# A fused two-layer transformer block: the place of the global-key products in the second attention, and the identity products behind them

## The chip, the cores and the metric

The kernel is one program on one core of a Trainium2 chip. The metric is the device time of one execution in microseconds, median of the runs. The engines named below are TensorE (PE, matrix products), VectorE (DVE), ScalarE (ACT), GpSimd (POOL) and SyncE (SP, which issues transfers). Each runs its own list of instructions in order and waits on semaphores that the other engines raise.

## The reference

The input is 16 batches of 256 tokens with 128 features. Four stages follow each other, each with a residual and a layernorm behind it:

```python
x = _layernorm(x + _L0_attn_ref(x, ...))   # 16 heads of 8, rotary, causal
x = _layernorm(x + _L0_ffn_ref(x, ...))    # one of 8 experts (diagonal weights)
x = _layernorm(x + _L1_attn_ref(x, ...))   # the stage that is changed
x = _layernorm(x + _L1_ffn_ref(x, ...))    # two of 8 experts, hidden width 512
```

The second attention has two parts for each of the 16 heads. Each query attends to the keys within 32 positions of it, and, in a softmax of its own, to 25 global keys, whose positions are an input (`global_indices`):

```python
local = softmax(Q Kwindow * scale) Vwindow
Kg, Vg = K[:, global_indices], V[:, global_indices]
glob = softmax(Q Kg * scale) Vg
out = (0.7 * local + 0.3 * glob) @ Wo.T + bo
```

## The kernel before

Both attentions are built by the same functions (`attention_pe`, `attention_act`, `attention_dve`, `attention_pool`, `attention_sp`), with `L.local` true for the second. Its order is written out by hand and unrolled: one iteration i per batch, from -1 to 19, and the iterations overlap. In iteration i the kernel prepares batch i+1 (projection, splitting, stacks of queries and keys), finds the score maxima of batch i (`pass1` on PE, `maxima` on DVE), computes and exponentiates the scores of batches i-1 and i (`pass2` on PE, `exp` on ACT, masks on POOL), multiplies by the values (`pv`), and finishes batch i-2 (`round_ot`, `round_og`, output projection, residual, layernorm). From iteration 4 on, two iterations share the routing of four tiles for the last stage: the even one does the choices on DVE (`chosen`, `both_choices`, L732 to L750), the odd one begins with `round_rp` on PE (L319, L322), which waits for `both_choices`, and with `positions` on DVE, which waits for `round_rp`.

An iteration has four steps j, one for every four heads, and each step has four units u. In unit (j, u) PE does `pass1`(j, u) (two matmuls, L348), then whatever round is due, then `pass2`(j, u), then `pv`(j, u-1). In unit (3, 3) the round is `round_mx(3)` (L172), `pass2` is the scores of the global keys (L372) and `pv` is their product with the values (L404).

The global keys of batch i+1 are picked out of the split keys by `round_kg` (L296): four pairs of matmuls with a selection matrix as the moving operand, 26 columns wide. It needs bank 1 of the two banks that all rounds share, so it waits for the last reader of this bank: ACT's copy of the second key stack, `keep_stack(1, 1)` (L521), which ACT does behind `exp`(3, 2). DVE copies the result to three places (`keep_kg`, L630 twice and L631 once) and raises `kg_kept`. The first `pass1` of the next iteration waits for that.

Behind `round_kg` stands `keep_array_busy` (L331): four fp32 products of the identity with itself, each two passes in the trace, into a bank of scores whose content is no longer needed. They wait for the maxima of unit (3, 2). Their result is read by nobody.

At the start of an iteration ACT copies the output banks (`keep_pv`, L485 and L487), which waits for the last `pv` of the iteration before; PE's `round_ot` (L168) in unit (0, 1) waits for the first of the two copies. ACT's first `exp` of the iteration (L536) comes behind both.

Of the kernel before, what the change touches and what calls it, by code (L numbers as in the profile page):

```python
# [15 lines left out]
P = 128  # L16
# [120 lines left out]
def wait(eng, sem, value):  # L137

    if not isinstance(value, int) or value > 0:
        eng.wait_ge(sem, value)  # L140
# [23 lines left out]
def attention_pe(pe, L, T, W):  # L164


    def turn(out, in_):
        return pe.transpose(out, in_, T.ident[:])  # L168
# [5 lines left out]
    def in_iteration(name, i, p, th):  # L174

        if name in ("og", "vg", "kg", "rt", "rl", "rp") and not L.local:
            return False
        if name in ("rt", "rl", "rp"):
            return th.pair and p == (name == "rp")
        if name in ("ot", "og", "ont", "y"):  # L180
            return th.finish
        if name[:2] == "mx":
            return th.max_step(int(name[2]))
        return th.scores if name == "vg" else th.turn_x if name == "xt" else th.prep
# [28 lines left out]
    def body(i, p, th):  # L213
# [21 lines left out]
        def round_xt(batch, par):  # L235
            if not (isinstance(batch, int) and batch == 0):
                bank_read("xt", i, p, th)
            pe.wait_ge(L.x_in[par], L.x_base + 8 * (batch - par) + 16)
            for tau in range(2):
                m = turn(T.mi[0][:, tau * P:(tau + 1) * P], T.xin[:, par, tau, :])  # L240
            m.then_inc(L.xt_done, 1)
# [8 lines left out]
        def round_pj(tau):  # L250
            bank_read(f"pj{tau}", i, p, th)
            pe.wait_ge(L.xt_kept, i + 2)
            m = pe.matmul(T.mi[tau][:, 0:3 * D], T.xt[:, tau * P:(tau + 1) * P], W.qkv[:], start=True, stop=True)  # L253
            m.then_inc(L.pj_done, 1)

        def round_ont():
            bank_read("ont", i, p, th)
            pe.wait_ge(L.on_done, fin + 1)
            for tau in range(2):
                m = turn(T.mi[0][:, tau * P:(tau + 1) * P], T.on[:, tau, :])  # L260
            m.then_inc(L.ont_done, 1)
# [29 lines left out]
        def round_kg():  # L291
            bank_read("kg", i, p, th)
            pe.wait_ge(L.ts_done, 2 * (i + 1) + 2)
            for t in range(4):
                for kt in range(2):
                    m = pe.matmul(T.mi[1][:, t * 32:t * 32 + NGE], T.tsr[:, kt, (4 + t) * P:(5 + t) * P],  # L296
                                  T.pick[:, kt, :], start=t == 0 and kt == 0, stop=kt == 1, skip_group_check=True)
            m.then_inc(L.kg_done, 1)
# [25 lines left out]
                              start=False, stop=True, skip_group_check=True)  # L324
            m.then_inc(L.rp_done, 2)

        def keep_array_busy():

            wait(pe, L.red_done, L.units * (4 * i + 3) + 3)
            for _ in range(4):  # L330
                pe.matmul(T.s1[0][:, 0:P], T.ident[:], T.ident[:], start=True, stop=True)  # L331

        def pass1(j, u):
            unit = L.units * (4 * i + j) + u
            bank = T.s1[u % L.ring1]
# [95 lines left out]
        for j in range(4):  # L431
            for u in range(L.units):
                if th.scores:
                    pass1(j, u)
                if j == 0 and u == 0 and in_iteration("rp", i, p, th):
                    round_rp()
                if j in (0, 1) and u == 0 and th.prep:
                    round_pj(j)
                if j == 0 and u == 1 and th.finish:
                    round_ot()  # L440
                if j == 0 and u == 2 and th.finish and L.local:
                    round_og()
                if j == 1 and u == (1 if L.local else 0) and th.finish:
                    round_ont()
                if j == 1 and u == 2 and in_iteration("rt", i, p, th):
                    round_rt()
                if j == 2 and u == 1 and L.local and th.scores:
                    round_vg()
                if j == 2 and u == 2 and in_iteration("rl", i, p, th):
                    round_rl()  # L450
                if j == 2 and u == 0 and th.finish:
                    round_y()
                if j == 3 and u in (0, 2) and th.prep:
                    round_stack(1, u // 2)
                if j == 3 and u == 0 and th.turn_x:
                    round_xt(i + 2, p)
                if u == L.units - 1 and th.max_step(j) and not (L.local and j == 0):
                    round_mx(j)
                if th.pass2[j]:
                    pass2(j, u)  # L460
                if th.late and u > 0:
                    pv(j, u - 1)
            if j in (1, 2) and th.prep:
                round_stack(0, j - 1)
            if L.local and j == 0 and th.max_step(j):
                round_mx(j)
        if L.local and th.prep:
            round_kg()
            keep_array_busy()

    iterations(pe, L.local, body)


# [102 lines left out]
def attention_dve(dve, L, T, W, x_all_in=None):  # L576


    def body(i, p, th):
# [44 lines left out]
        def keep_kg():  # L624


            dve.wait_ge(L.kg_done, i + 2)
            kg = T.mi[1][:, 0:4 * 32].rearrange("p (t g) -> p t g", t=4)
            for lo in (0, NGE + S):
                dve.tensor_copy(T.ks[n][:, :, lo:lo + NGE], kg[:, :, 0:NGE])  # L630
            dve.tensor_scalar(T.kg[n][:, :, 0:NG], kg[:, :, 0:NG], T.rows[:, 0:1], None,  # L631
                              ALU.add).then_inc(L.kg_kept, 1)
# [25 lines left out]
        def maxima(j, u):  # L658

            step = 4 * i + j  # L660
            bank = T.s1[u % L.ring1]
            if u == 0:
                wait(dve, L.msp_done, step - 1)
            wait_apart(dve, L.passed, L.p1_done, L.units * step + u + 1)
            nm = T.nm[:, j % 2, 0, :]

            def masked_maximum(item, at, mask):

                return dve.tensor_tensor_reduce(at, at, mask, -1.0, -BIG, ALU.add, ALU.min, nm[:, item:item + 1])  # L669

            if L.local:
                for c in range(2):
                    item = 2 * u + c
                    lo = c * WG + (0 if item // 4 else NGE)
                    masked_maximum(item, bank[:, lo:lo + WIN], T.band[:, item // 4, :])
                lo = 0 if u < 2 else WIN
                m = dve.tensor_reduce(T.nm[:, j % 2, 1, 2 * u:2 * u + 2],  # L677
                                      bank[:, 0:2 * WG].rearrange("p (h k) -> p h k", k=WG)[:, :, lo:lo + NG],
                                      AX.X, ALU.max, negate=True)
            elif u == 0:  # L680
                for t in range(4):
                    m = masked_maximum(t, bank[:, t * P:(t + 1) * P], T.causal[:, P:S])
            else:
                for c in range(2):
                    m = masked_maximum(2 + 2 * u + c, bank[:, c * S:(c + 1) * S], T.causal[:, :])
            m.then_inc(L.red_done, 1)
# [96 lines left out]
        for j in range(4):  # L783
            for u in range(L.units):
                if th.scores:
                    maxima(j, u)
                if second_half and j == 0:
                    if u == 0:
                        positions()
                    if u == 1:  # L790
                        places()
                    if u == 3:
                        weights_of_choices()
                if first_half:
                    if (j, u) == (2, 3):
                        logits()
                        best_of(T.best[:, :], 1)
                    if (j, u) == (3, 0):
                        chosen(0, 4)
                        without_first()  # L800
                    if (j, u) == (3, 1):
                        best_of(T.best2[:, :], 7)
                    if (j, u) == (3, 3):
                        chosen(1, 10)
                        both_choices()
                if j in (0, 1) and u == 0 and th.prep:
                    keep_pj(j)
                if j == 0 and u == L.units - 2 and th.finish:
                    normalise()
                if j == 2 and u == (2 if L.local else 0) and th.finish:  # L810
                    residual()
                if j == 2 and u == 1 and L.local and th.scores:
                    keep_vg()
                if j == 3 and u == 2 and th.finish:
                    layernorm()
        if L.local and th.prep:
            keep_kg()

    iterations(dve, L.local, body)

# [1231 lines left out]
```

## Time and profile before

| what | value |
|---|---|
| median of 3 runs | 1143.39 us (1137.0, 1143.39, 1153.99) |
| the profiled execution's own time | 1135.99 us |
| its span, first to last instruction | 1134.2 us |
| PE busy in the span | 960.8 us (85%) |
| DVE, POOL, ACT busy | 770.9, 666.2, 579.3 us |
| second attention | from about 450 to about 905 us of the span |

The times in the rows below are microseconds from the start of the span, durations microseconds (ns only where marked). A timeline row gives the start, the length, the engine, the line, the operation and how many instructions were merged; in brackets the idle time before it and what ended it. Lengths of matmuls overlap, because they are pipelined: the cost of a group is the distance from its start to the start of the next group.

### The profile page before, as it was taken

To read this page: it belongs to the slowest core of one execution; us is meant where nothing else is said; L and a number is where in the kernel's file an instruction comes from. 1 tells how busy PE (TensorE), PEld (TensorE's weight loads), DVE (VectorE), ACT (ScalarE), POOL (GpSimd) and SP (SyncE) were. 2 spreads that over 40 slices of the span, in tenths; PEclk is the share of its full clock that TensorE was granted. 3 is DMA by queue.
4 is the path that set the end of the run, shared out by engine and by line. 5 is a ranking of instruction groups with operands and counts; after the bars stand their busy time and mean duration, and the time that the engine had idled before them with its cause. 6 is when DMAs were issued, how large, how long until landed. Compare 5 with 4: busy or idle time off the path is not lost.

```text
span 1134.2 us, 27975 instructions
## 1 busy us (share of the span) xinstructions
PE 960.8 (85%) x7664; PEld 711.1 (63%) x7664; DVE 770.9 (68%) x3598; ACT 579.3 (51%) x1250; POOL 666.2 (59%) x1493
## 2 busy tenths in 40 slices
PE   3899999999959995899999999999999419999930
PEld 2667777777735552777777777777776318888720
DVE  3877778788826785567677767677775327777736
ACT  2566666666622332355555455554545107777724
POOL 3566666566632222267668787787778522565556
PEclk8999999999978998599999999999999559999965
DMA  6111111211032432111112121211211157777636
GB/s 179 37 40 44 29 44 29 48 25 44 22 132 95 179 125 84 44 32 28 47 30 57 37 55 45 63 42 55 58 33 35 45 166 230 238 256 249 207 96 163
DMA packets 71377, 98.36 MB, mean 87 GB/s; under 512 B 13689, under 2 KB 43257, under 8 KB 71105
## 3 DMA queue, kind: packets, MB, share of 16 engines
q1 hardware_dynamic: 61040, 83.31, 25.0%
q0 software_dynamic: 4992, 10.30, 2.6%
q10 hardware_dynamic: 5232, 3.42, 1.2%
q8 instruction: 50, 0.82, 0.3%
q14 instruction: 63, 0.51, 0.1%
HBM read 49.48 MB, written 24.77 MB: 65 GB/s over the span
## 4 chain that ended last, share of the span: by engine, by line
PE 71%; DVE 11%; issue 5%; DMA 4%; POOL 3%; ACT 3%; SPq 2%; ACTq 0%; DVEq 0%; POOLq 0%
PE bank L348 6%; PE bank L172 5%; PE bank L253 4%; PE bank L357 4%; PE bank L378 4%; PE bank L1262 4%; PE bank L412 3%; PE bank L168 3%; PE bank L419 3%; PE bank L1496 3%; PE bank L1497 3%; PE bank L1498 3%; PE bank L352 3%; PE bank L387 3%; PE bank L404 3%
## 5 line engine op out<-in xcount | busy, mean ns | idle before, releaser
L536 ACT ACTIVATE p<-bank 128x480 f32<-128x480 f32 (+1 forms) x448 | 239.8, 539 | 271.8 <-PE bank L378 108.4
L669 DVE CUSTOM_DVE_ANT_0 bank<-bank,band 128x160 f32<-128x160 f32 x512 | 156.8, 347 | 91.8 <-PE bank L348 90.2
L669 DVE CUSTOM_DVE_ANT_0 bank<-bank,causal 128x128 f32<-128x128 f32 (+1 forms) x512 | 169.4, 386 | 65.3 <-PE bank L352 51.8
L898 POOL TENSOR_SCALAR_AFFINE_SELECT p<-p 128x380 f32<-128x380 f32 (+1 forms) x256 | 146.3, 601 | 75.7 <-ACT p L536 74.9
L669 DVE DVE_READ_ACCUMULATOR2_ANT nm<- 128x1 f32 x1024 | 143.9, 141 | 0.1
L1675 POOL DMA_INDIRECT y_rows<-p,rows x92 | 90.1, 979 | 83.6 <-DVE p L1622 61.9
L879 POOL TENSOR_SCALAR_AFFINE_SELECT p<-p 128x256 f32<-128x256 f32 (+1 forms) x192 | 90.7, 484 | 64.2 <-ACT p L536 60.9
L348 PE MATMUL bank<-ks,qs 128*128 128x186 f32 x512 | 117.2, 313 | 1.3 <-DVE nm L677 1.1
L348 PEld LDWEIGHTS bank<-ks,qs 128*128 128x128 f32 x512 | 80.4, 198 | 34.0 <-issue 19.3
L378 PE MATMUL bank<-qs,ks 128*128 128x160 f32 x512 | 101.0, 300 | 0.0
L1617 DVE TENSOR_TENSOR ks<-p,ts 128x512 fp32r<-128x512 f32 x92 | 63.9, 694 | 28.4 <-ACT ts L1570 26.7
L1567 ACT ACTIVATE p<-bank,wb 128x512 f32<-128x512 f32 x92 | 63.6, 691 | 37.9 <-PE bank L1498 35.6
L928 POOL DMA_INDIRECT xr<-xs,placei x64 | 65.0, 1016 | 27.1 <-DVE xs L779 15.2
L378 PEld LDWEIGHTS bank<-qs,ks 128*128 128x128 f32 x512 | 75.2, 193 | 7.5
L172 PE MATMUL bank<-identr,ts 128*128 128x128 f32 x512 | 71.0, 265 | 8.0 <-POOL ts L869 6.5
L172 PEld LDWEIGHTS bank<-identr,ts 128*128 128x128 f32 x512 | 55.2, 146 | 20.8 <-issue 12.4
L1262 PE MATMUL bank<-p,expert 128*128 128x512 f32 x128 | 67.0, 607 | 0.7 <-DVE p L1321 0.7
L412 PE MATMUL bank<-p,vb 128*32 128x160 f32 x1024 | 61.3, 311 | 1.1 <-POOL vb L835 0.6
L357 PE MATMUL bank<-ks,qs 128*128 128x256 f32 x256 | 61.9, 325 | 0.3 <-DVE nm L669 0.3
L253 PE MATMUL bank<-w_qkv,xt 128*128 128x384 f32 x128 | 59.6, 553 | 1.0 <-ACT xt L492 1.0
L352 PE MATMUL bank<-ks,qs 128*128 128x128 f32 x256 | 42.0, 288 | 19.3 <-ACT ks L521 14.7
L357 PEld LDWEIGHTS bank<-ks,qs 128*128 128x128 f32 x256 | 39.1, 193 | 26.2 <-issue 24.5
(209 smaller groups left out, 2370.0 us busy)
## 6 DMA issues: line engine op xcount, KB each, us to landing
qs<-parts SPq DMA_DIRECT2D x46, 512.0 KB, 5.2
qs<-qf SPq DMA_DIRECT2D x128, 128.0 KB, 2.4
rows<-xr SPq DMA_DIRECT2D x23, 260.0 KB, 3.2
parts<-ks SPq DMA_DIRECT2D x8, 512.0 KB, 2.7
xs<-x_b SPq DMA_DIRECT2D x16, 256.0 KB, 2.9
p<-in_w SPq DMA_DIRECT2D x12, 256.0 KB, 3.2
xin<-in_x SPq DMA_DIRECT2D x16, 128.0 KB, 2.2
parts<-qf SPq DMA_DIRECT2D x4, 512.0 KB, 2.7
```

The source lines that it names most:

```text
L172: return pe.transpose(out.bitcast(F32R), in_, T.identr[:])
L253: m = pe.matmul(T.mi[tau][:, 0:3 * D], T.xt[:, tau * P:(tau + 1) * P], W.qkv[:], start=True, stop=True)
L348: m = pe.matmul(bank[:, c * WG:(c + 1) * WG], q[:, t, tau * P:(tau + 1) * P], k[:, t, lo:lo + WG], start=c == 0, stop=True, skip_group_che ...
L357: m = pe.matmul(bank[:, c * S:(c + 1) * S], q[:, t, P:S], k[:, t, NGE:NGE + S], start=c == 0, stop=True, skip_group_check=True)
L378: m = pe.matmul(bank[:, c * WIN:(c + 1) * WIN], k[:, t, NGE + kt * P:NGE + (kt + 1) * P], q[:, t, lo:lo + WIN], start=c == 0, stop=True, s ...
L412: m = pe.matmul(T.ov[32 * t:32 * t + 32, lo:lo + WIN], T.vb[n][:, part, j, t, :], flat[:, item * WIN:(item + 1) * WIN], start=j == 0 and p ...
L536: act.activation(pb[:, :, :].rearrange("p u c -> p (u c)")[:, lo:lo + cols], bank[:, 0:cols], ACT.Exp, scale=SCALE).then_inc(L.exp_done, 1)
L669: return dve.tensor_tensor_reduce(at, at, mask, -1.0, -BIG, ALU.add, ALU.min, nm[:, item:item + 1])
L879: pool.affine_select(out=at, in_=at, compare_op=ALU.is_ge, fill=0.0, base=0, pattern=[[0, heads], [1, P]], channel_multiplier=-1).then_inc ...
L898: pool.affine_select(out=at, in_=at, compare_op=ALU.is_ge, fill=0.0, base=base, pattern=[[0, 4], [sign, hi - lo]], channel_multiplier=-sig ...
L1262: pe.matmul(T.yb[p][:, :], W.expert[:, e * D:(e + 1) * D], T.xm[e % 4], start=e == 0, stop=e == E - 1).then_inc(M.y_done, 1)
L1675: pool.indirect_dma_start(Z.y_dram[:, :], bass.IndirectOffsetOnAxis(ap=rows[:, a, C_GOAL:C_GOAL + 1].bitcast(I32), axis=0), Z.ys[r][:, a * ...
```

## The change

Three things change, all in the second attention. PE's `round_kg` moves from the end of the iteration into unit (3, 3), behind `pass1`(3, 3) and ahead of `round_mx(3)`, `pass2`(3, 3) and `pv`(3, 2). DVE's `keep_kg` moves from the end of the iteration to the place right behind `maxima(3, 3)`; in the even iterations from 4 on this is ahead of `chosen` and `both_choices`, in all others nothing stood between. `keep_array_busy` is removed. No transfer is added, removed or moved, and the lists of ACT, POOL and SP stay as they are.

```diff
-        def keep_array_busy():
-
-            wait(pe, L.red_done, L.units * (4 * i + 3) + 3)
-            for _ in range(4):
-                pe.matmul(T.s1[0][:, 0:P], T.ident[:], T.ident[:], start=True, stop=True)
 ...
                 if j == 3 and u == 0 and th.turn_x:
                     round_xt(i + 2, p)
+                if L.local and (j, u) == (3, 3) and th.prep:
+                    round_kg()
                 if u == L.units - 1 and th.max_step(j) and not (L.local and j == 0):
                     round_mx(j)
                 if th.pass2[j]:
 ...
-        if L.local and th.prep:
-            round_kg()
-            keep_array_busy()
 ...
                 if th.scores:
                     maxima(j, u)
+                if L.local and (j, u) == (3, 3) and th.prep:
+                    keep_kg()
 ...
-        if L.local and th.prep:
-            keep_kg()
```

## Rows read from the trace of the kernel before

**Rows 1.** Page: granted TensorE clock in 40 slices, tenths of full speed.
```profile
PEclk8999999999978998599999999999999559999965
```

**Rows 2.** Windows: busy time per engine (instructions), granted clock, DMA share, GB/s.
```profile
640.00:740.00 100.00, 96.51 (x918) 72.12 (x919) 73.22 (x434) 53.84 (x128) 80.69 (x200) 0.98 0.18 50
```

**Rows 3.** Waits of PE from 480 to 880: total us, times, longest.
```profile
PE bank L172 <- DVE logits L719: 7.1, 6, 1.2
PE bank L172 <- DVE on L610: 3.0, 15, 0.3
```

**Rows 4.** Timeline of PE, end of iteration 5 and start of 6.
```profile
603.02 0.47 PE L348 MATMUL bank<-ks,qs 128*128 128x186 f32 x2
603.32 0.28 PE L172 MATMUL bank<-identr,msp 128*16 128x128 f32 x2
...
604.45 1.15 PE L296 MATMUL bank<-pick,ts 128*128 128x26 f32 x8
605.45 1.14 PE L331 MATMUL bank<-ident 128*128 128x128 f32 x8
606.40 0.44 PE L348 MATMUL bank<-ks,qs 128*128 128x186 f32 x2
...
607.88 0.49 PE L168 MATMUL bank<-ident,ovs 128*128 128x128 f32 x3
```

**Rows 5.** Timeline of ACT, the same stretch.
```profile
603.05 0.59 ACT L521 CAST ks<-bank 128x512 fp32r<-128x512 f32 x1
...
604.84 0.58 ACT L485 COPY ovs<-bank 128x512 f32<-128x512 f32 x1
605.32 0.59 ACT L487 COPY ogs<-bank 128x512 f32<-128x512 f32 x1
607.85 0.57 ACT L536 ACTIVATE p<-bank 128x480 f32<-128x480 f32 x1 [1.94 <-PE bank L378]
```

**Rows 6.** Timeline of DVE, the same stretch.
```profile
604.75 0.20 DVE L677 TENSOR_REDUCE nm<-bank 128x2 f32<-128x50 f32 x1
605.63 0.44 DVE L630 CAST ks<-bank 128x104 fp32r<-128x104 f32 x2 [0.69 <-PE bank L296]
605.99 0.31 DVE L631 TENSOR_SCALAR kg<-bank,rows 128x100 f32<-128x100 f32 x1
```

**Rows 7.** Timelines of DVE and PE, end of iteration 4 (even).
```profile
579.08 0.20 DVE L677 TENSOR_REDUCE nm<-bank 128x2 f32<-128x50 f32 x1
...
579.79 0.24 DVE L749 TENSOR_TENSOR both<-picks 128x32 f32<-128x32 f32 x1
577.62 0.47 PE L348 MATMUL bank<-ks,qs 128*128 128x186 f32 x2
...
581.28 0.33 PE L319 MATMUL bank<-both,tri 128*128 128x32 f32 x2
```

**Rows 8.** Timeline, end of iteration -1 (the array at half clock).
```profile
462.04 0.31 DVE L631 TENSOR_SCALAR kg<-bank,rows 128x100 f32<-128x100 f32 x1
...
463.20 0.71 PE L348 MATMUL bank<-ks,qs 128*128 128x186 f32 x2
```

**Rows 9.** Timeline, end of iteration 0.
```profile
480.39 0.58 ACT L521 CAST ks<-bank 128x512 fp32r<-128x512 f32 x1
...
481.02 1.06 PE L296 MATMUL bank<-pick,ts 128*128 128x26 f32 x8
```

**Rows 10.** Windows, columns as in rows 2: two stretches with waits.
```profile
624.00:628.00 4.00, 3.48 (x20) 2.23 (x21) 1.04 (x8) 1.09 (x3) 3.64 (x11) 0.58 0.01 5
868.00:872.00 4.00, 3.38 (x39) 2.32 (x39) 1.68 (x5) 2.12 (x5) 3.71 (x13) 1.00 0.47 135
```

**Rows 11.** Timeline of PE: identity products ending iterations 6, 7 and 8.
```profile
633.63 1.14 PE L331 MATMUL bank<-ident 128*128 128x128 f32 x8
658.99 1.14 PE L331 MATMUL bank<-ident 128*128 128x128 f32 x8
685.97 1.14 PE L331 MATMUL bank<-ident 128*128 128x128 f32 x8
```

## The prediction

> **What bounds the kernel now.** I read the page's slices first: between the second expert stage and the last one the granted clock stands at 9 tenths or more for some ten slices, and drops to 5 at either end [rows 1]. That plateau is the second attention. The windows over it show why: in 100 us PE is busy for 96.51, POOL for 80.69, DVE for 73.22, ACT for 53.84 [rows 2]. So in this stage PE's own list of instructions is the bound, and a product that is taken off the list is worth its full distance to the next one, unless PE then has to stand still for another engine. The waits of PE confirm it: from 480 to 880 there are two kinds that repeat, 7.1 us in 6 waits and 3.0 us in 15 [rows 3], some 10 us in 400. Both are answered by DVE chains that start from PE's own `pass1`, so they move along with PE and neither swallow nor return a gain.
>
> **The identity products.** In steady state they start at 605.45 and the next `pass1` at 606.40 [rows 4]: 0.95 us for the group, 16 groups in the trace (iterations -1 to 14). DVE copies the keys during them: it ends at 605.99 + 0.31 = 606.30 [rows 6], 0.10 us before the `pass1`. So the identity products cover the copy, and taking them out alone would win about 0.1 us a batch. The gain hangs on the other half of the change.
>
> **The moved products, on PE.** I count from s, the start of `pass1`(3, 3), here 603.02. In the old order `round_mx(3)` starts at s+0.30, the key products at s+1.43, the identity products at s+2.43, the next `pass1` at s+3.38 [rows 4]. In the new order the key products want to start at s+0.30. They need the copy of the second key stack, which ACT runs from 603.05 for 0.59 us [rows 5], until s+0.62. PE follows about 0.05 us behind such an end: at iteration 0 the copy ends at 480.39 + 0.58 = 480.97 and the key products start at 481.02 [rows 9]. So they start at s+0.67, and PE stands for up to 0.37 us that it did not stand before. Queued behind this wait are `round_mx(3)`, `pass2`(3, 3) and `pv`(3, 2). The key products take 1.00 us (604.45 to 605.45), the three behind them 1.13 us (603.32 to 604.45) [rows 4]. The next `pass1` could be at s+0.67+1.00+1.13 = s+2.80. That is 0.58 us earlier than now. The bounds of this term: if ACT's copy came first there would be no wait and the gain would be 0.95; if the copy is as late as in iteration 0, nothing is left.
>
> **The keys' copy, on DVE.** The first copy starts 605.63 - 604.45 = 1.18 us behind the start of the key products and the last one ends 0.67 us later [rows 4, 6], so in the new order at s+0.67+1.18+0.67 = s+2.52. The maxima of unit (3, 3) end at 604.95, s+1.93 [rows 6], and the copies behind them at s+2.60 at the latest. Both are ahead of s+2.80, so `pass1` does not wait for `kg_kept`. The margin is 0.2 to 0.3 us. It is the new cover: the maxima row, `pass2` and `pv` in place of the identities.
>
> **Even iterations from 4 on.** Here `chosen` and `both_choices` stand behind the copies. Now they run from the end of the maxima, 579.28, to 580.03: 0.75 us. In the new order they run from s+2.52 (maxima end at s+1.66) to about s+3.3, with wake-ups s+3.4. `round_rp` started at s+3.66 (581.28 less 577.62) [rows 7] and would be ready at s+3.08. It stands for about 0.3 us, and of the 0.58 some 0.25 is left. There are six of these (4, 6, ..., 14). What is behind `round_rp` on PE, the projection and `pass2`(0, 0), moves with it.
>
> **The ends.** At iteration -1 the key products are in the same place and only the identities go. DVE ends at 462.35 and `pass1` starts at 463.20 [rows 8]; it can start near 462.40: 0.8 us, at half clock. At iteration 0 the key products already start at the end of ACT's copy [rows 9]; the copies on DVE then end 1.85 us later at 482.87, about where `pass1` starts now. I count 0.05.
>
> **What loses slack and costs nothing.** `pv`(3, 2) is the last product of the iteration, and ACT's copies of the output banks wait for it. In the old order it ended a little before 604.84, the first copy ran then for 0.58, and `round_ot` came at 607.88 [rows 4, 5]: 2.5 us to spare. In the new order `pv` ends 1.37 us later and `round_ot` comes 0.58 us earlier, which leaves about 0.5. Likewise ACT is free for `exp`(0, 0) at 605.91 now and waits 1.94 us for it [rows 5]; 1.94 - 1.37 - 0.58 is zero. Both covers still hold, by little. If they went, the cost would be tenths of a microsecond in eight batches. No transfer is moved; the row of maxima that SyncE sends for `round_mx(3)` leaves 1.3 us later and is needed only in step 1 of the next iteration. The wait of the identity products for the maxima of (3, 2) goes too, but the next `pass1` has the same wait.
>
> **The sum.** 8 x 0.58 = 4.6 (iterations 1, 2, 3, 5, 7, 9, 11, 13), 6 x 0.25 = 1.5, 0.8 and 0.05: 7.0 us. The profiled execution took 1135.99; by the sum it would take 1129. The median of the runs is 7.4 us above it, and the four times shown (with the profiled one) have their middle at 1140.2. I take that middle: 1140.2 - 7.0 = 1133.
>
> **Clock: rule against row.** In the trace the array falls to its lower level (1.2 of 2.4 GHz) at times behind DVE's long wait: the window at 624 has a granted clock of 0.58 [rows 10], and the iteration with it takes 28.18 us from identity to identity (605.45 to 633.63), where the same kind without a fall takes 26.98 (658.99 to 685.97) [rows 4, 11]. A fall costs 1.2 us. The stretch at 868, where PE is idle for 0.6 of 4 us in pieces, keeps a clock of 1.00 [rows 10], and so do the fifteen short waits of 0.2 to 0.3 us [rows 3]. The new waits (0.37 and 0.3) are of this size, so I count no new falls. The Trainium skill, TensorE: Matmul & The Clock Gate, section "A second HAM failure mode: psum-queue depth-cycling", speaks against the change: it says that a PE which idles for moments between groups of matmuls, often enough, has its clock swing between the two levels and pays for each swing. By that rule the second rival below would be the likely one. The trace, with its fifteen short waits and no fall at them, does not agree with it at this size of wait.
>
> **Rivals.** (1) The forecast above, 1133: chance 0.57. (2) Slower: the clock falls at the batch boundary. The wait of 0.37 us and 1.0 us of products only 26 columns wide follow each other, and no identities of 128 columns come behind. Price 1.2 us a fall. It decides from six falls on, which eat the 7.0; at all 15 boundaries with scores it is +18 - 7 = +11, so 1151. For it: the old order never has a wait right before the narrow products. Against it: the rows just told. Chance 0.17. (3) A wait takes the gain: ACT's copy comes later (as in iteration 0), or `pass1` waits for `kg_kept` as DVE is late behind a layernorm. Then the 0.58 shrinks to 0.1 or 0.2 and the sum is about 3 us or less: 1137 to 1140. For it: margins of 0.2 us. Against: the rows of one boundary recur nearly to the hundredth. This is also the case in which the change does not do what it says. Chance 0.17. (4) More: PE waits for nothing new, 15 x 0.95 + 0.8 = 15 us, or some of the old falls vanish too (1.2 each): 1125 to 1130. Chance 0.09.
>
> **Numbers.** The range has to take in the executions' own spread, 1136 to 1154 before the change, as well as the cases: from 1125 (case 4) to 1151 (case 2). A difference of 2% is 23 us, about what a measurement of this kernel can tell from no change. No case reaches it: faster would take the whole of case 4 and a lucky median, 0.04; slower would take some 25 falls, 0.04; within 2%: 0.92.
>
> **What would show it.** Right: the interval from `pass1`(3, 3) to the next `pass1` is 2.8 us in place of 3.38; L296 follows L348 after about 0.67 us with an idle time ended by ACT's L521; L319 shows a wait of some 0.3 us for L749 in six iterations; PE's busy time is some 16 us lower, and the span only some 7. Wrong: `pass1` waits for L631, the granted clock falls between iterations, or `round_ot` waits for L485. The forecast is wrong as a whole if the stage's time between two boundaries does not fall by 0.2 to 0.6 us in iterations without a clock fall.

## The result: 1.9% slower, and the profile after

| | before | after |
|---|---|---|
| median of 6 runs | 1143.46 us | 1163.45 us |
| lowest, highest | 1136.31, 1153.99 | 1160.04, 1198.72 |
| ratio after to before | | 1.0194, 95% interval 1.0138 to 1.025 |
| profiled execution, span | 1134.2 us | 1158.7 us |
| mean granted clock over the span | 0.920 | 0.903 |

Ratios leave disturbed executions out, medians here and below hold all of them, so the two can give different distances (in e10 below 16 and 25 us). The forecast was 1133 with a range up to 1151: the time went the other way and lies outside the range. In the changed kernel the line numbers are lower: `pass1` L342, `pass2` of the global keys L366, `pv` L398 and L406, ACT's key copy L513, `both_choices` L741; `round_kg` is still L296.

The page's clock row, beside that of before [rows 1]:

```profile
PEclk9999999999979996699888799888999659999975
```

The plateau of the second attention now has sixes, sevens and eights in it. A stretch in which the granted clock is at its lower level, 1.2 of 2.4 GHz, is called a fall; the batch boundary is the stretch from `pass1`(3, 3) to the first `pass1` of the next iteration. Two windows give it as one number: first the second attention of the kernel before, from its first to its last `pass1`, then that of the changed kernel (columns as in rows 2).

```profile
463.20:865.60 402.40, 389.73 (x3643) 293.99 (x3643) 291.48 (x1746) 208.16 (x493) 294.06 (x766) 0.97 0.16 43
```
```profile
462.41:886.20 423.79, 407.77 (x3522) 301.74 (x3522) 291.75 (x1748) 208.53 (x493) 295.50 (x766) 0.89 0.15 41
```

The stage is 21.4 us longer (423.8 less 402.4) with 121 matmuls fewer in the records; PE's busy time rose by 18 us, DVE, ACT and POOL do what they did. The granted clock went from 0.97 to 0.89. Summed over windows of 2 us, the full-speed time lost to the clock (length times one less the clock, "clock loss" from here on) is 12.4 us before and 45.0 after. The span grew by 24.5; the other 3 us lie outside the stage, where the loop of the last stage alone took 5 us longer (144.9 against 140.0 us). That is not the change's: e10, the changed kernel again, has 139.1.

The batch boundary itself went as the diff says. Timeline of PE in the changed kernel, end of iteration 9 (columns as in rows 4):

```profile
722.99 0.47 PE L342 MATMUL bank<-ks,qs 128*128 128x186 f32 x2
723.65 1.06 PE L296 MATMUL bank<-pick,ts 128*128 128x26 f32 x8 [0.20 <-issue]
724.57 0.28 PE L172 MATMUL bank<-identr,msp 128*16 128x128 f32 x2
...
725.70 0.55 PE L342 MATMUL bank<-ks,qs 128*128 128x186 f32 x2
726.17 0.91 PE L253 MATMUL bank<-w_qkv,xt 128*128 128x384 f32 x2
```

From `pass1`(3, 3) to the next `pass1` it is 2.71 us; it was 3.38 [rows 4]. The iteration's length at full clock, from 700.69 to 725.70, is 25.01 us; the odd iterations of before take 25.37. So each boundary is shorter, and the stage is longer. Windows of the changed kernel around the end of iteration 6 show where it goes:

```profile
628.00:632.00 4.00, 2.75 (x32) 2.04 (x24) 3.35 (x22) 0.81 (x2) 3.56 (x6) 0.87 0.05 17
632.00:636.00 4.00, 4.00 (x25) 2.83 (x24) 0.86 (x5) 1.21 (x3) 3.11 (x10) 0.50 0.04 10
636.00:640.00 4.00, 4.00 (x25) 3.26 (x24) 2.56 (x19) 1.80 (x4) 0.54 (x1) 0.50 0.63 148
640.00:644.00 4.00, 4.00 (x29) 2.68 (x28) 2.23 (x14) 0.92 (x2) 3.14 (x12) 0.50 0.00 0
644.00:648.00 4.00, 4.00 (x19) 3.61 (x16) 1.24 (x9) 1.70 (x4) 1.17 (x2) 0.50 0.16 54
648.00:652.00 4.00, 4.00 (x23) 3.04 (x22) 2.15 (x13) 0.88 (x2) 0.00 (x0) 0.57 0.03 6
```

PE stands for 1.25 us in the first window: the old wait for DVE's choices. In the unit ahead of it stand the router's products, 8 columns wide, so that narrow products and a wait come close together here as at the new boundary (timeline of PE in the changed kernel):

```profile
628.41 1.02 PE L311 MATMUL bank<-router,xrt 128*128 128x8 f32 x8
...
630.06 0.46 PE L342 MATMUL bank<-ks,qs 128*128 128x186 f32 x2
631.77 0.38 PE L172 MATMUL bank<-identr,msp 128*16 128x128 f32 x2 [1.25 <-DVE logits L711]
```

Then the clock falls to its lower level and stays there for 20 us although PE shows 4.00 busy of 4.00. In the kernel before such a fall was over after some 3.5 us [rows 10]. The changed kernel has eight falls between 480 and 884: two of 20 us, one of 10, two of 7, three of 3.5. Five of them start in unit (2, 3), at or just behind the old wait for the choices, and three at the boundary, behind the moved key products. The kernel before had three of 3.5, all of which start in unit (2, 3).

The waits of PE from 480 to 900 in the changed kernel (columns as in rows 3):

```profile
PE bank L172 <- DVE logits L711: 7.3, 6, 1.2
PE bank L172 <- DVE on L602: 2.9, 14, 0.3
PE bank L296 <- ACT ks L513: 2.2, 8, 0.8
PE bank L296 <- issue: 1.0, 5, 0.2
...
PE bank L319 <- DVE both L741: 0.2, 1, 0.2
```

New are the waits ahead of the key products, 3.2 us in 13. As idle time they cannot carry 21 us. The wait for `both_choices`, forecast for six iterations, occurs once.

### The profile page after: what moved, and what is told of

It reads as the page before. It is cut to its first block, busy times and chain, and to the rows that moved or that the text cites. A ratio compares the mean times of both kernels' runs of the same rounds, so it can differ in the third digit from the quotient of the medians.

```text
span 1158.7 us, 27719 instructions
## 1 busy us (share of the span) xinstructions
PE 978.0 (84%) x7536; PEld 715.8 (62%) x7536; DVE 769.9 (66%) x3598; ACT 578.3 (50%) x1250; POOL 670.6 (58%) x1493
## 3 DMA queue, kind: packets, MB, share of 16 engines
q1 hardware_dynamic: 61040, 83.31, 24.5%
## 4 chain that ended last, share of the span: by engine, by line
PE 69%; DVE 11%; issue 7%; ACT 4%; POOL 3%; SPq 3%; DMA 2%; another core or an unknown queue 1%; ACTq 0%; DVEq 0%; POOLq 0%
PE bank L342 6%; PE bank L172 5%; PE bank L253 4%; PE bank L372 4%; PE bank L351 4%; PE bank L1254 3%; PE bank L168 3%; PE bank L413 3%; PE bank L1488 3%; PE bank L1490 3%; PE bank L406 3%; PE bank L1489 3%; PE bank L346 3%; PE bank L381 3%; PE bank L398 3%
## 5 line engine op out<-in xcount | busy, mean ns | idle before, releaser
L1667 POOL DMA_INDIRECT y_rows<-p,rows x92 | 92.5, 1005 | 87.2 <-DVE p L1614 60.7
L342 PE MATMUL bank<-ks,qs 128*128 128x186 f32 x512 | 124.2, 328 | 2.3 <-DVE nm L669 1.4
L342 PEld LDWEIGHTS bank<-ks,qs 128*128 128x128 f32 x512 | 86.1, 208 | 38.6 <-issue 22.7
L372 PE MATMUL bank<-qs,ks 128*128 128x160 f32 x512 | 107.9, 316 | 0.0
L372 PEld LDWEIGHTS bank<-qs,ks 128*128 128x128 f32 x512 | 81.0, 206 | 9.2 <-issue 3.0
L253 PE MATMUL bank<-w_qkv,xt 128*128 128x384 f32 x128 | 63.4, 585 | 1.1 <-ACT xt L484 1.0
L406 PE MATMUL bank<-p,vb 128*32 128x160 f32 x1024 | 63.2, 320 | 0.9 <-POOL vb L827 0.5
L381 PE MATMUL bank<-qs,ks 128*128 128x256 f32 x256 | 55.8, 299 | 0.0
```

What stands on the lines that cost most here:

```text
L342: m = pe.matmul(bank[:, c * WG:(c + 1) * WG], q[:, t, tau * P:(tau + 1) * P], k[:, t, lo:lo + WG], start=c == 0, stop=True, skip_group_che ...
L372: m = pe.matmul(bank[:, c * WIN:(c + 1) * WIN], k[:, t, NGE + kt * P:NGE + (kt + 1) * P], q[:, t, lo:lo + WIN], start=c == 0, stop=True, s ...
L406: m = pe.matmul(T.ov[32 * t:32 * t + 32, lo:lo + WIN], T.vb[n][:, part, j, t, :], flat[:, item * WIN:(item + 1) * WIN], start=j == 0 and p ...
L1667: pool.indirect_dma_start(Z.y_dram[:, :], bass.IndirectOffsetOnAxis(ap=rows[:, a, C_GOAL:C_GOAL + 1].bitcast(I32), axis=0), Z.ys[r][:, a * ...
```

## The experiments

Two theories. **C**, clock: the identity products kept the array active; without them the clock falls more often and stays down longer. **S**, schedule: the new order puts work behind waits on PE and DVE, and that costs the time. All runs are in groups on one chip with the kernel before beside them. The expectations give absolute times, those of e1, e2, e3 and e6 for a kernel before of some 1143 us, the others for some 1135; where the kernel before of the group took another time, they are read as distances from it.

| run | median us | before, median | ratio (95% interval) | clock loss, stage us (one profile) | median clock of the runs |
|---|---|---|---|---|---|
| e10, changed kernel again | 1159.71 | 1134.98 | 1.0144 (1.0106 to 1.0182) | 52.1, 429.9 | 0.896 |
| e1, before without products | 1149.15 | 1136.49 | 1.0113 (1.0079 to 1.0148) | 50.2, 433.4 | 0.909 |
| e2, moved, products at the end | 1151.71 | 1136.49 | 1.0140 (1.0103 to 1.0176) | 22.9, 417.5 | 0.915 |
| e3, moved, products ahead of the keys | 1137.12 | 1136.49 | 1.0015 (0.9989 to 1.0042) | 25.1, 413.5 | 0.922 |
| e6, before, products 8 columns wide | 1143.67 | 1136.49 | 1.0072 (1.0046 to 1.0099) | 29.1, 417.4 | 0.914 |
| e4, before, choice waits filled | 1130.70 | 1134.98 | 0.9958 (0.9941 to 0.9976) | 5.0, 397.8 | 0.932 |
| e5, changed, choice waits filled | 1134.38 | 1134.98 | 0.9977 (0.9951 to 1.0003) | 13.4, 398.8 | 0.922 |
| e9, changed, two ahead, filled | 1127.52 | 1134.98 | 0.9936 (0.9913 to 0.9959) | 7.6, 394.5 | 0.927 |
| e12, changed, filled 8 columns wide | 1161.95 | 1143.47 | 1.0101 (1.0029 to 1.0173) | 44.8, 423.6 | 0.895 |
| e8, before without products, filled | 1147.26 | 1143.47 | 1.0045 (1.0008 to 1.0082) | 20.5, 410.6 | 0.919 |
| e11, changed, four ahead, filled | 1142.96 | 1143.47 | 0.9958 (0.9915 to 1.0001) | 9.6, 402.1 | 0.931 |

The median clock of the kernel before in the three groups was 0.926 (e1, e2, e3, e6), 0.925 (e10, e4, e5, e9) and 0.923 (e12, e8, e11). The profiles of e1, e3, e6, e8 and e10 fell on executions of 1169.3, 1149.6, 1150.1, 1153.8 and 1165.0 us, which lie 20, 12, 6, 7 and 5 us above their medians. Above all in e1 and e3 the clock of the profile (0.891 and 0.911) is lower than in a usual execution of the kernel, so the last column is the one to compare.

**e1: take the products out, move nothing.**

```diff
             round_kg()
-            keep_array_busy()
```

> The kernel before with the identity products left out and nothing moved. Theory C (clock): without them TensorE's clock falls at batch boundaries and stays down longer; the clock time lost in the second attention rises from 5 us at full speed (three falls of 3.4 us) to 20 to 40, and the time is 10 to 22 us above the kernel before (1153 to 1165). Theory S (schedule: the new waits at the moved key products and on VectorE cost the time): nothing is moved here, so the time is that of the kernel before less about 1 us (1142), since VectorE's copy covers all but 0.1 us of the products.

Measured: 1.0113. This is 13 us above before, as C has it (10 to 22), and S is excluded as the whole cause, as no instruction is moved. The full-clock iterations show that the products cost nothing where they stood. In the timeline of PE in e1 at the end of iteration 5 the distance from `pass1` to `pass1` is 3.38 as before; the time of the products has become waiting. The second fence, of the waits of PE from 480 to 895, shows this at all 15 boundaries:

```profile
607.38 0.46 PE L348 MATMUL bank<-ks,qs 128*128 128x186 f32 x2
...
608.81 1.15 PE L296 MATMUL bank<-pick,ts 128*128 128x26 f32 x8
610.76 0.43 PE L348 MATMUL bank<-ks,qs 128*128 128x186 f32 x2 [0.81 <-issue]
```
```profile
PE bank L348 <- issue: 13.0, 15, 1.2
```

And a window of the same execution (at 1169.3 us the second slowest of e1), in which the clock is down nearly throughout with PE busy for 22.05 of 24 us:

```profile
796.00:820.00 24.00, 22.05 (x119) 16.84 (x118) 10.71 (x66) 6.86 (x16) 10.08 (x27) 0.51 0.14 36
```

**e2: keep the moves, products at the end of the iteration.**

```diff
             if L.local and j == 0 and th.max_step(j):
                 round_mx(j)
+        if L.local and th.prep:
+            keep_array_busy()
```

> The changed kernel with the four identity products put back at the end of the iteration (the moves stay). Theory C: the falls go back to about three, the boundary from pass1(3,3) to the next pass1 is 2.71 + 0.95 = 3.66 us against 3.38 before, so the time is 2 to 5 us above the kernel before (1145 to 1149). Theory S: the moves are what costs, so it stays at 1160 or above.

Measured: 1.0140, 15 us, against 2 to 5 expected by C. The time met neither theory: it is 10 us above C's, and S wanted 1160 or above. The boundary is 3.71 us (3.66 expected); that is about 5 us of work over 15 boundaries. The rest goes with the clock: 0.915 against 0.926, and the profile has falls that touch the boundaries of iterations 0, 4 and 12. The longest, 17 us, starts at the wait for the choices of iteration 12. So products in the old place do not make up for the moved keys. That it is their distance from the narrow key products and from the wait ahead of them is argued and not shown.

**e3: keep the moves, products ahead of the keys.**

```diff
                 if L.local and (j, u) == (3, 3) and th.prep:
+                    keep_array_busy()
                     round_kg()
```

> The changed kernel with the four identity products put ahead of the moved key products in unit (3, 3), where 0.37 us of them fill the wait for ScalarE's copy. Theory C: few falls, boundary 0.30 + 0.95 + 1.00 + 1.13 = 3.38 us as before, time within 4 us of the kernel before (1140 to 1147). Theory S: as the changed kernel, 1160 or above. If falls come back although the products are there, their place right behind the narrow products is what counts.

Measured: 1.0015, no difference from before. With the products in the wait, the moved keys, the new order on DVE and the later copies on ACT are all still there, and the 20 us are gone. S falls with this run. The boundary is 3.16 us (3.38 expected), and the odd iterations take 25.41 (before 25.37). The profile, of an execution 12 us above the median, still has a fall of 20 us. It starts at the wait for the choices of iteration 14 and runs through the boundary, wide products and all:

```profile
844.00:848.00 4.00, 3.33 (x23) 2.53 (x23) 1.33 (x10) 1.21 (x3) 3.64 (x11) 0.69 0.01 4
848.00:852.00 4.00, 4.00 (x25) 3.31 (x24) 2.87 (x21) 1.62 (x3) 0.94 (x2) 0.50 0.64 148
...
860.00:864.00 4.00, 4.00 (x20) 3.96 (x19) 1.88 (x15) 0.88 (x2) 0.00 (x0) 0.50 0.01 4
864.00:868.00 4.00, 4.00 (x36) 2.56 (x36) 2.55 (x13) 1.23 (x4) 1.46 (x3) 0.75 0.03 6
```

**e6: the old kernel, products 8 columns wide.**

```diff
-                pe.matmul(T.s1[0][:, 0:P], T.ident[:], T.ident[:], start=True, stop=True)
+                pe.matmul(T.s1[0][:, 0:8], T.ident[:], T.ident[:, 0:8], start=True, stop=True)
```

> The kernel before with the identity products cut from 128 to 8 moving columns (8 of the identity's columns, same number of instructions, same place). If what keeps the clock is that the array works on many columns (theory C in its strict form), the falls come as in the changed kernel: 1153 to 1165. If it is enough that TensorE executes something, or if the schedule is the cause (S), it stays at 1140 to 1145, like the kernel before.

Measured: 1.0072, between the two cases. The iterations at full clock are as before (26.98, 25.37 us), so the 7 us are clock. It leaves open whether narrow products at the boundary help by half or not at all: its interval overlaps that of e1. e12 asks the same in the other place.

**e10: the changed kernel again.** No edit.

> The changed kernel once more, on the chip of this group, for its clock and span run by run. Theory C (clock): about 20 to 27 us above the kernel before, and over the runs of both kernels the time goes up by 0.7 us for each microsecond of full-speed clock time lost; at equal loss the changed kernel is 4 to 7 us faster. Theory S (schedule): at equal loss it is still 10 us or more slower.

Measured: 1159.71 against 1134.98, 25 us in the medians and 16 by the ratio (C expected 20 to 27). That the changed kernel is slower holds on another chip. The clock loss over the whole span has a median of 120.4 us against 85.0 for before, 35.4 more. Over the six runs of this kernel the time goes up by 0.89 us per microsecond of clock loss (0.71 over the first six), and over the 24 of before by 0.52, over the 17 of the other group by 0.71. In the stage alone, e10 and e5 (below) differ in little but the clock, as e5's added products stand in waits: (429.9 - 398.8) / (52.1 - 13.4) = 0.80. With 0.8, a clock loss of 35.4 us costs 28, and the measured 24.7 would leave a gain of 3 to 4 us at equal clock, where C expected 4 to 7. This estimate hangs on the slope: with 0.52 it is a loss of 6 us, with 0.89 a gain of 7. e5 against e4, below, measures the gain without it.

**e4 and e5: fill the waits for the choices**, in before and in the changed kernel.

```diff
+        def fill_choice_wait(n):
+            wait(pe, L.red_done, L.units * (4 * i + 2) + 3)
+            for _ in range(n):
+                pe.matmul(T.s1[0][:, 0:P], T.ident[:], T.ident[:], start=True, stop=True)
 ...
+                if (j, u) == (2, 3) and th.scores and in_iteration("rl", i, p, th):
+                    fill_choice_wait(4)
                 if u == L.units - 1 and th.max_step(j) and not (L.local and j == 0):
                     round_mx(j)
```

> The kernel before, with four more identity products (0.95 us) in the six waits of 1.1 to 1.2 us in unit (2, 3) of the even iterations, where TensorE stands for VectorE's choices. They write a score bank whose maxima are done. Theory C: the falls that begin at these waits go away (three in the trace of before, 1.2 us each): 1 to 6 us faster than the kernel before (1131 to 1135). Theory S: idle time of TensorE does not matter, no change.

> The changed kernel with the same four products in the same six waits; the batch boundary stays without products. Theory C: the falls that begin at the waits, and run on through the boundary for up to 20 us, go away; those that begin at the boundary itself (three in the trace) stay: 8 to 18 us faster than the changed kernel, still 3 to 15 us above the kernel before. Theory S: as the changed kernel.

Measured: e4 0.9958, 4.3 us faster than before, and its profile has no fall between 480 and 880 (one of 7 us from 472). e5 0.9977: 25 us faster than the changed kernel in the medians, 19 by the ratios, where C expected 8 to 18, by products in six waits that lie elsewhere. Timeline of PE in e5, unit (2, 3) of iteration 6; the wait for L719 shrinks from 1.2 to 0.32 us:

```profile
629.99 0.47 PE L348 MATMUL bank<-ks,qs 128*128 128x186 f32 x2
630.29 1.08 PE L331 MATMUL bank<-ident 128*128 128x128 f32 x8
631.69 0.28 PE L172 MATMUL bank<-identr,msp 128*16 128x128 f32 x2 [0.32 <-DVE logits L719]
631.91 0.64 PE L372 MATMUL bank<-qs,kg 128*32 128x256 f32 x8
```

e4 and e5 have all iterations from 2 to 14 at full clock, so they give the schedule's gain cleanly: 23.86 against 24.25 us in iteration 3, 25.01 against 25.37 in the odd and 26.61 against 26.98 in the even ones, 0.37 a batch. Still the medians order them the other way (1134.4, 1130.7): e5's clock is 0.922 against 0.932, and its profile has a fall of 10 us that starts at the boundary of iteration 0. At the other 14 boundaries with scores none starts.

**e12: the same fill, 8 columns wide.**

```diff
-                pe.matmul(T.s1[0][:, 0:P], T.ident[:], T.ident[:], start=True, stop=True)
+                pe.matmul(T.s1[0][:, 0:8], T.ident[:], T.ident[:, 0:8], start=True, stop=True)
```

> The changed kernel with four products in the waits for the choices, as in the run before, but 8 moving columns wide in place of 128. If the array's activity (columns) is what holds the clock, the falls at these waits stay and the time is 10 to 25 us above the kernel before (1145 to 1160). If any executed matmul holds it, the time is that of the changed kernel with wide products in the waits, within 2 us of the kernel before (1133 to 1137).

Measured: 1161.95, 18 us above before in the medians and 12 by the ratio (interval 3 to 20), as the activity case has it (10 to 25). The median clock, 0.895, is that of the changed kernel without any fill (0.896); with the wide fill it was 0.922. Timeline of PE in e12, the same unit:

```profile
636.24 0.47 PE L348 MATMUL bank<-ks,qs 128*128 128x186 f32 x2
636.54 1.13 PE L331 MATMUL bank<-ident 128*128 128x8 f32 x8
637.91 0.38 PE L172 MATMUL bank<-identr,msp 128*16 128x128 f32 x2 [0.24 <-DVE logits L719]
638.23 1.08 PE L372 MATMUL bank<-qs,kg 128*32 128x256 f32 x8
```

and its windows over the same stretch:

```profile
636.00:640.00 4.00, 3.76 (x31) 2.34 (x23) 2.39 (x14) 1.00 (x3) 3.38 (x10) 0.65 0.01 2
640.00:644.00 4.00, 4.00 (x26) 3.66 (x28) 1.69 (x11) 1.66 (x4) 1.45 (x3) 0.50 0.33 78
...
652.00:656.00 4.00, 4.00 (x16) 3.39 (x16) 1.63 (x9) 0.69 (x2) 0.00 (x0) 0.50 0.19 60
656.00:660.00 4.00, 4.00 (x35) 3.18 (x34) 2.58 (x18) 1.67 (x4) 0.63 (x2) 0.79 0.00 0
```

The narrow products occupy PE as long as the wide ones (1.13 and 1.08 us in the profile) and leave as short a wait (0.24 and 0.32), and the clock falls all the same and stays down for 20 us. So in these waits busy time in the profile does not hold the clock, and the width of the products does.

**e8: before without the boundary products, waits filled.** The edits of e1 and e4 together.

> The kernel before without the identity products at the batch boundary, with four wide products in the waits for the choices. Theory C with a start and a continuation (falls start at the waits for the choices, and the products at the boundary end them early): filling the waits leaves few starts, so the missing boundary products cost little: 1130 to 1136, against 1149 without the fill. If falls start at the boundary as often: 1140 to 1150.

Measured: 1.0045, 1147.26, 3.8 us above before in its group, which itself was 7 to 8.5 us slower than the other two groups. As a distance from before it lies between the two cases. Its profile has the second one's falls: one of 10 us and five of 3.5, all starting within 2.6 us behind the first `pass1` after a boundary, where e4, with the products, has none. Filling the waits removes the long falls of e1 but not the starts at the boundary, where e8 has key products of 26 columns and a wait of 0.81 us behind them. One of the six, at the end of iteration 6, in a timeline of PE and a window:

```profile
641.38 1.15 PE L296 MATMUL bank<-pick,ts 128*128 128x26 f32 x8
643.33 0.43 PE L354 MATMUL bank<-ks,qs 128*128 128x186 f32 x2 [0.81 <-issue]
```
```profile
644.00:648.00 4.00, 4.00 (x21) 3.40 (x20) 2.36 (x15) 0.57 (x1) 0.79 (x1) 0.60 0.11 33
```

**e9 and e11: the better version.** Changed kernel, fill of e5, and two or four wide products ahead of the key products.

```diff
                 if L.local and (j, u) == (3, 3) and th.prep:
+                    keep_array_busy(2)   # e11: 4
                     round_kg()
```

> The changed kernel with two identity products (0.48 us) ahead of the moved key products, where 0.37 us is a wait, and the four in the waits for the choices. Theory C: boundary about 2.9 us (before 3.38), few falls: 2 to 8 us faster than the kernel before, if two products are enough to hold the clock; between the two kernels if not. Theory S: 1160 or above.

> As the best version so far (moved key products, products ahead of them, waits for the choices filled), with four products ahead in place of two. Boundary 3.16 us in place of 2.72, so 15 x 0.44 = 6.6 us more work if the two already hold the clock: 1133 to 1135. If the two leave falls that four would prevent: 1128 or below.

Measured: e9 0.9936, 7.5 us faster than before, and 32 us (by the ratios 24) faster than the changed kernel in its group: it beats both. About 6 of the 7.5 us are what the moved keys save at full clock (below), so this is mostly the schedule's gain, with the clock held. Against e5, which lacks only the two products, it is 7 us faster. Timeline of PE in e9 (here `pass1` is L354), end of iteration 7:

```profile
653.26 0.47 PE L354 MATMUL bank<-ks,qs 128*128 128x186 f32 x2
653.56 0.63 PE L331 MATMUL bank<-ident 128*128 128x128 f32 x4
653.95 1.04 PE L296 MATMUL bank<-pick,ts 128*128 128x26 f32 x8
...
655.98 0.55 PE L354 MATMUL bank<-ks,qs 128*128 128x186 f32 x2
```

The boundary is 2.72 us, that of the changed kernel (2.71): the two products stand wholly in the wait for ACT's copy. e11's boundary is 3.16. Its median clock is 0.931 against 0.923 for before in its group (e9 0.927 against 0.925), its stage takes 402.1 us against 394.5, and its ratio 0.9958 (0.9915 to 1.0001) lies 0.2% above e9's, 2.5 us where 6.6 were expected; the intervals overlap, so the order of the two is not settled.

## Why the prediction was wrong

**What bounds the kernel: right.** PE's list is the bound, and its time per product is the time. That is also why the clock weighs so much: 0.8 us of stage time for each microsecond of clock loss.

**The schedule steps: right in kind, 0.4 instead of 0.58 and 0.25.** The key products start at s+0.66 (s+0.67 forecast), the next `pass1` at s+2.71 (s+2.80). Behind it stands 0.2 us that I had not: L253 follows 0.47 us behind `pass1` and not 0.28. In the even iterations the wait for `both_choices` (0.3) does not appear, since DVE's copies start 0.1 us earlier than taken and the routing steps behind them take 0.74 us. What remains is 0.37 us a batch in all kinds (e5 against e4), about 5.3 us over iterations 1 to 14, and the 0.8 at iteration -1, where `pass1` now starts 0.09 us behind the copy [rows 8]. The sum was 7.0; by these it is about 6. The covers that were to hold by little held: `round_ot` waits for no copy in these iterations.

**The step that failed: "I count no new falls".** The forecast put this term at nothing; the stage's clock loss went from 12.4 to 45.0 us, in eight falls for three. I asked only whether the new waits would start one, and priced a fall at 1.2 us from a kernel in which falls were short. First, falls do start at the changed boundary: three of the eight. The fifteen short waits without a fall [rows 3] stood ahead of products of 128 columns, not ahead of 26-column ones. Second, the old waits for the choices start falls anyway, three of six before and five of six after, and a fall from there has no fixed length. In the changed kernel two of the five run 20 us, through the next boundary, and one of 7 us is followed by one of 10 over the boundary; the other two last 3.5. Together the falls cost some 26 us (0.8 times 32.6), less a gain of about 5, which is the 21.4 by which the stage grew. e1 shows that missing products alone cost clock and time, e3 that the moves with products ahead of them do not, and e5 that without the starting waits nearly all of the loss is gone.

**What ends a fall is not shown.** In the kernel before, the three falls were over some 5 us ahead of the boundary's products: the first ends at 628.0, the products start at 633.63 [rows 11]. So these products did not end them. Over the profiles of all runs, 31 falls start in unit (2, 3). The 14 that start within 1.5 us behind its `pass1`, before the wait there ends, last 7 to 27 us; of the 17 that start later, 16 last 3.5 us and one, in e3, 20. The one profile of the kernel before has only late ones. How much of the lengthening is owed to the missing products, and how much to the place in the wait at which a fall happened to begin, these traces do not separate. That the products hold the clock rests on the clock over all runs (0.926 to 0.909 in e1) and on the starts at the boundary (six in e8, none in e4 from 480 to 880).

**The rivals.** Rival 2 named the clock and its reason, the missing wide products behind a wait and narrow products, with 0.17. It had the place by less than half, as five of the eight falls start at the old waits, and its size (+11) was too small, as the price of 1.2 us a fall was. The Trainium skill's rule in TensorE: Matmul & The Clock Gate, section "A second HAM failure mode: psum-queue depth-cycling", that small idle times between groups of matmuls make the clock swing, was weighed and set aside. By that rule, the trace of the changed kernel agrees, with eight falls for three. The rule speaks of idle time only; in e12 the narrow products left the clock where the bare waits had left it (0.895 and 0.896).

**What stays open.** Whether a given wait starts a fall varies between executions and batches (three of six waits before), and no run shows what decides it. Why the products protect the boundary ahead of the keys (e3) and hardly at the end of the iteration (e2) is argued from their distance to the narrow products and not shown. The gain of the moved keys at equal clock is read from one profile each of e4 and e5. The last stage's loop takes 138.4 to 140.0 us in some profiles and 143.2 to 145.5 in others (changed kernel, e12, e8, e11) with the same code, so the first comparison's 5 us there are not the change's.

## What to carry to other kernels

Before products without a reader are deleted, ask what the clock does without them; test the deletion alone, and read the granted clock per window, not PE's busy time. If a kernel is bound by TensorE, put wide idle products into waits that exist anyway, ahead of narrow products: there they cost nothing (2.72 against 2.71 us at the boundary). Here they bring 0.4% to the kernel before (e4), and to the changed kernel 1.6% in the waits for the choices (e5) and 0.4% more ahead of the keys (e9). A short fall in one kernel is no price for a fall in another, as a fall of the same wait lasted 3.5 us in one iteration and 20 in another.

## What the runs showed of the hardware

At half clock, a PE with 4.00 of 4.00 us busy does not get its clock back by that alone: 20 us in the changed kernel, and 24 in e1 with PE busy for 22.05. In waits of 1.2 us, eight fp32 passes of 8 columns take PE 1.13 us in the profile and of 128 columns 1.08 us, and only the wide ones raise the clock over the runs: 0.895 (e12) and 0.922 (e5), with ratios to before of 1.0101 and 0.9977. Short waits decide over it: with six of 1.2 us filled with wide products, the profile of the kernel before has no fall in place of three, and the time is 0.4% lower (e4). A fall that starts early in such a wait lasted 7 to 27 us (14 cases), one that starts later 3.5 (16 of 17).
